# Large neighbour aggregation: ScalarE's Abs in two halves, with the second copy of a tile between them

## The reference, cut to what matters

```
thr = mean - std                       # of the distances to the half-rolled image
xj = 0
for axis in (rows, columns):
    for s in range(0, size, K):        # K = 4 at level 0, 2 at the others
        xr = roll(x, s, axis)
        dist = sum over channels |x - xr|
        m = dist < thr
        xj = maximum(xj, (xr - x) * m)
```

## Time and profile before

| | us |
|---|---|
| median of 3 timed runs | 8505.98 |
| the profiled execution | 8487.06 |
| its span, first to last instruction | 8485.2 |
| PE busy | 5984.2 |
| DVE busy | 5096.2 |
| ACT busy | 4346.2 |
| POOL busy | 3214.9 |

### The profile page before, as it was taken

The page is one execution under the profiler, slowest core; times in us unless marked ns, Lnnn a source line. Parts: engine busy times, 40 slices in busy tenths (PEclk is TensorE's granted clock), DMA queues, the critical chain, the costliest instruction groups (busy, mean ns, idle before and its releaser), DMA issues. The chain is left out here.

```text
span 8485.2 us, 82873 instructions
## 1 busy us (share of the span) xinstructions
PE 5984.2 (71%) x26092; PEld 2959.6 (35%) x26286; DVE 5096.2 (60%) x5868; ACT 4346.2 (51%) x4790; POOL 3214.9 (38%) x1140
## 2 busy tenths in 40 slices
PE   7896577667776676985676432363998849889798
PEld 5673111111111111334111111252886627666263
DVE  2111799899999898650799654224222223459596
ACT  1123699899999898750899311101001121125657
POOL 0161799899999897000898031000000000000000
PEclk9998899999999999998999766586999979999898
DMA  6567330111211101667000322255547879984545
GB/s 124 131 199 238 59 40 20 40 60 21 40 20 25 65 30 35 192 160 145 24 11 1 105 45 50 42 90 157 103 85 126 149 188 170 188 171 126 181 124 186
DMA packets 1476784, 841.70 MB, mean 99 GB/s; under 512 B 638754, under 2 KB 1406264, under 8 KB 1462664
## 3 DMA queue, kind: packets, MB, share of 16 engines
q1 hardware_dynamic: 1261032, 717.18, 36.9%
q10 hardware_dynamic: 215456, 120.95, 6.0%
HBM read 533.33 MB, written 304.65 MB: 99 GB/s over the span
## 5 line engine op out<-in xcount | busy, mean ns | idle before, releaser
L1025 POOL TENSOR_TENSOR ag_D<-ag_X 128x2048 f32<-128x2048 f32 (+15 forms) x940 | 2907.7, 3127 | 1060.9 <-DMA ag_X<-h 941.8
L1089 PE MATMUL ag_slot<-ag_S,ag_w 128*128 128x512 bf16 x4768 | 1470.7, 389 | 838.7 <-DVE ag_J L1131 720.9
L1131 DVE TENSOR_TENSOR ag_J<-ag_J,ag_slot 128x1024 f32<-128x1024 f32 x1240 | 1454.7, 1214 | 153.4 <-PE ag_slot L1089 72.9
L1138 DVE SCALAR_TENSOR_TENSOR ag_J<-ag_slot,ag_J 128x1024 f32<-128x1024 f32 (+14 forms) x1640 | 1436.4, 928 | 0.0
L1056 ACT ACTIVATE ag_slot<-ag_D 128x1024 f32<-128x1024 f32 x1280 | 1308.5, 1025 | 173.8 <-DVE ag_J L1138 58.9
L1040 ACT ACTIVATE ag_A<-ag_D 128x2048 f32<-128x2048 f32 x640 | 1212.1, 1894 | 0.0
L1089 PEld LDWEIGHTS ag_slot<-ag_S,ag_w 128*128 128x128 bf16 x4960 | 286.5, 98 | 2256.7 <-DVE ag_J L1131 1299.8
L1082 PE MATMUL ag_dist<-ag_A,ag_given 128*32 128x512 f32 x5120 | 698.5, 618 | 101.6 <-ACT ag_A L1040 77.6
L255 PE MATMUL dc_ps<-dc_high,dc_w_high 128*128 128x512 f32 (+1 forms) x1056 | 425.2, 403 | 281.2 <-DVE dc_low L68 281.2
L1048 ACT ACTIVATE ag_S<-ag_dist,ag_limit 128x512 bf16<-128x512 f32 x640 | 486.7, 761 | 2.3 <-PE ag_dist L1082 2.3
L269 ACT ACTIVATE dc_out<-dc_ps,shift,scale 128x512 f32<-128x512 f32 (+1 forms) x88 | 67.4, 766 | 818.2 <-PE dc_ps L255 818.2
(11 more groups left out here) (208 smaller groups left out, 9521.9 us busy)
## 6 DMA issues: line engine op xcount, KB each, us to landing
ag_X<-h SPq DMA_DIRECT2D x18, 2048.0 KB, 13.3
xj<-ag_J SPq DMA_DIRECT2D x18, 2048.0 KB, 7.2
c_mul<-gated SPq DMA_DIRECT2D x64, 512.0 KB, 11.5
wa_x<-r SPq DMA_DIRECT2D x128, 256.0 KB, 2.9
u<-wa_x SPq DMA_DIRECT2D x128, 256.0 KB, 2.4
mn_x<-u SPq DMA_DIRECT2D x64, 512.0 KB, 5.7
cpe_band<-in_band SPq DMA_DIRECT2D x16, 1792.0 KB, 8.0
gr_hj<-h SPq DMA_DIRECT2D x168, 128.0 KB, 2.8
```

The source lines that it names most:

```text
L1025: pool.tensor_tensor(self.tile_part(self.d[u % self.DEPTH][:], u, piece), self.span(g, axis, there, there + hi - lo), self.span(g, axis, l ...
L1089: mm = self.nc.tensor.matmul(self.slot[v % self.SLOTS][:, b, :], self.w[:, weights + 2 * h + b, :], self.s[u % 3][:], start=False, stop=Tr ...
L1131: dve.tensor_tensor(best, best, new, ALU.max).then_inc(self.dve_steps, 1)
L1138: dve.scalar_tensor_tensor(out=best, in0=self.slot_part(v, lo, hi), scalar=-1.0, in1=best, op0=ALU.mult, op1=ALU.max)\
```

## The change

ScalarE's Abs becomes two ACTIVATEs of 1024 elements. In `act_unit` the first goes ahead of the second copy, the second behind it. Each half keeps the waits of the whole and counts up the semaphore `absed` by one, and TensorE's distance waits for both.

```diff
-            self.act_abs(act, u)
+            self.act_abs(act, u, 0)
+            self.act_abs(act, u, 1)
...
-    def act_abs(self, act, u):
+    def act_abs(self, act, u, h):
         act.wait_ge(self.diffed, self.diffs_to[u])
         reach(act, self.summed, u - 2)
-        act.activation(self.a[u % 3][:], self.d[u % self.DEPTH][:], ACT.Abs).then_inc(self.absed, 1)
+        part = slice(h * self.SUB, (h + 1) * self.SUB)
+        act.activation(self.a[u % 3][:, part], self.d[u % self.DEPTH][:, part], ACT.Abs).then_inc(self.absed, 1)
...
         self.act_copy(act, 2 * u + 1)
+        if u + self.LEAD < len(self.units):
+            self.act_abs(act, u + self.LEAD, 0)
         if u + 1 < len(self.units):
             self.act_copy(act, 2 * u + 2)
         if u + self.LEAD < len(self.units):
-            self.act_abs(act, u + self.LEAD)
+            self.act_abs(act, u + self.LEAD, 1)
         if u + 1 < len(self.units):
             self.act_sign(act, u + 1)
...
     def pe_dist(self, pe, u):
-        pe.wait_ge(self.absed, u + 1)
+        pe.wait_ge(self.absed, 2 * u + 2)
```

## The result

The median after the change is 8463.8 us (5 runs, 8454.7 to 8470.61); the kernel before, in five runs beside it, has 8507.99 (8499.84 to 8519.72). The ratio is 0.9946, 95% interval 0.9931 to 0.996: 44 us less, 8461 was predicted.

What follows compares the result with a forecast made beforehand. DVE was taken to wait 0.21 us a pair behind a loop through ScalarE's second copy and Abs. 150 row pairs x 0.14 plus 150 column pairs x 0.16 save 45 us: 8506 to 8461, range 8449 to 8500.

Steps and rivals of the forecast that it cites:

- DVE's hidden wait of 0.21 us: DVE's two plain rolls take 2.47 us a pair of units instead of 2.26; without waiting, 9.11 in rows, 9.18 in columns.
- The loop: Roll end, second copy, Abs, distance, pad, Max: 4.64 us, then 4.68 to the roll's end, setting the measured pair of 9.32.
- The price of a half: On ScalarE, half an Abs takes 1.04 us, holding a 0.945 us slot; a unit grows 0.09 to 4.44 us.
- The new loop: After the change, from the first copy's slot: 5.66 us to Max, then 3.48 or 3.55: 9.14 or 9.21 a pair.
- TensorE's order: Distance matmuls stand behind the two swaps, which wait for the second Max: 9.16 us a pair in rows, 9.23 in columns.
- POOL's floor: POOL's own pace in the large aggregations: 9.16 us a pair in rows, 9.22 in columns.
- The sum: 150 row pairs at 0.14 us and 150 column pairs at 0.16 us saved: 45 us.
- The borders: At chunk borders nothing changes: the second copy's vanished wait of about 0.1 us pays the halves' added 0.09.
- The signs of being wrong: Wrong if: half over 1.06 us or gaps; two rolls still 2.47; POOL's 2048-element difference slower; a border over 0.5 us longer.
- Partial saving: Rival: POOL slows under pressure or PE's order costs more; 0.08 us a pair, 24 us saved, 8482; chance 0.18.
- halves that eat the gain: Rival: second copy's wait goes but halves at 1.056 us without overlap eat it; 10 us saved, 8496; chance 0.15.
- ScalarE as the pace: Rival: ScalarE becomes the pace once both halves exceed 2.11 us; at a 1.26 slot 234 us slower, 8740; chance 0.12.

Runs made afterwards that it cites:

- e10: e2 with Abs first on ScalarE, ahead of both copies, and the distance first on TensorE, ahead of pad and swaps: 8428.01 us, ratio 0.9921.
- e1: The changed kernel with both halves of Abs behind the second copy: 8521.14 us, ratio 1.003 to the kernel before.
- e5: The changed kernel with each half of Abs cut again in place, the distance waiting for four: 8518.07 us, ratio 1.0021 to the kernel before.
- e9: The same kernel as e2, run on another chip: 8452.73 us, ratio 0.9939 to the kernel before.
- e7: e2 with POOL's one-piece differences computed over their first half only, from a stage's sixth unit on: 8446.72 us, ratio 0.9934.
- e11: e10 with the edit of e7, POOL's one-piece differences over their first half only: 8420.56 us, ratio 0.9915.
- e2: The kernel before with Abs in one piece moved ahead of the second copy: 8450.96 us, ratio 0.9943.

## Why the prediction was right

- **What bounds the kernel.** DVE's hidden wait of 0.21 us in every pair, read from starts alone, was right: e10, in which the wait is gone, has the 9.11 and 9.18 that were worked out for DVE.
- **The loop.** Roll end, second copy, Abs, distance, pad, Max is shown: its Abs made 0.09 longer made the pair 0.10 longer (e1), and the halves cut again cost 0.18 to 0.19 (e5). The new loop was put at 5.66 + 3.48 = 9.14 and, with the split roll, 9.21. The trace has slots of 0.96, 0.95 and 0.95 where 0.945 was taken, and 1108.02 - 1106.33 = 1.69 where 1.70 was: 0.02 more in all, 9.16 and 9.23.
- **The price of a half.** 1041 ns against 1.04 us. A further cut cost 0.09 us in e1 and in e5. The Trainium skill, page "ScalarE: Activation LUTs", section "What ACT_TABLE_LOAD costs", states 186 ns + 0.833 ns per element and an overlap of some 93 ns; estimated by it, a half takes 1039 ns and a further cut costs 186 - 93 = 93 ns. The traces agree with both.
- **What is late next.** Of the three floors, TensorE's order (9.16 and 9.23) was right: 9.17 and 9.24, with Abs out of the loop (e9) and with POOL relieved (e7); with the distance ahead of the swaps it goes (e10). POOL's floor was right in rows (9.18 in three chunks of e10, against 9.11 in e11) and too high in columns: 9.22 was read from a stretch where POOL waited for ScalarE's copies, and e10 runs columns at 9.18.
- **The sum.** 45 us was predicted, and the aggregations gave 39.8. I split that: the first 14 pairs with rolls of each pass, added up over the ten row passes, went from 1306.7 to 1294.6 us, so 12.1, where 140 x 0.14 = 19.6 was meant; over the column passes from 1314.7 to 1295.9, 18.8 for 140 x 0.16 = 22.4. In rows 7.5 us are missing: 3.2 in the second half of a pass, 9.24 where the sum had 9.18, and 3.4 in first pairs, three of which take 10.9 us where one did before (last section). The 3.6 missing in columns are for the most part one such first pair and five pairs of 9.51. The lone units, the last pairs and the borders gave the other 8.9, where I had counted 3.0 for the last pairs. The medians differ by 44 us, so the total came closer than its terms.
- **The borders.** They were called unchanged. Of the 8.9 us, 6.9 are lone units (188.1 to 181.2 over all passes): a stretch of lower clock that fell into them before falls into the first pair now in some passes, and is shorter or gone in others. Lone units and first pairs together went from 376.9 to 372.1 us, 4.8 less, of which the pairs' saving was to give 3.0. So the starts of passes are about even, but not one by one: some grew by up to 1.8 us, and others shrank by up to 1.4.
- **The signs of being wrong.** Two of those listed showed and yet decided nothing: POOL's difference of 2048 elements is 17 ns slower, but in e7 a POOL with idle time leaves the pair at 9.17; and some borders grew by more than 0.5 us, but the sum of all didn't grow.
- **The rivals.** Partial saving (8482) and halves that eat the gain (8496) lie outside the five runs. ScalarE as the pace was refuted by e5 more than by the time: with four Abs instructions a unit it still wasn't the pace.
- **What I hadn't asked.** The prediction took the split for the means of the gain. It is the order: e1, the split without the move, costs 0.3%, and e2, the move without the split, has the whole gain. So the prediction was right in the loop and in the time, and had too narrow a view of what takes Abs out of the loop.

## What to carry to other kernels

When three engines look full and the views of waits show nothing, add up the steps from start to start on the last engine, find the two equal instructions that take longer than their peers, and follow the start times back from there to a loop that closes. On an engine that works in order, first try another order: an instruction that can wait goes behind those that are ready and feed a longer chain, and a split, which costs 0.09 us a cut here, is for where no whole instruction can be moved. After each step compute what is late next, and check it by relieving that resource alone: e7 cleared POOL, and e10 then gained by reordering TensorE, and ScalarE with it.

## What the runs showed of the hardware

TensorE's granted clock falls to 0.50 at the start of most passes (18 of the changed kernel's 20, 19 of the 20 before), and the work beside it can take longer. Where it stays there over some 6 us of the first pair with rolls, that pair takes 10.9 us instead of 9.17 or 9.24: in 4 passes of the changed kernel and in 5 of e9 (10.9 to 11.0). The kernel before has one, but its clock falls earlier, in the lone units (a distance of 1.94 us at 2607.40, at a granted clock of 0.50), eight of which take 10.1 to 10.4 us where the others take 8.3 to 9.7. I can't tie it to the order of the work. TensorE alone, at the border of a column chunk of the changed kernel, and then the windows of the same stretch (the column before DMA share and GB/s is the granted clock, as a share of 2.4 GHz):

```profile
1840.62 1.07 PE L1086 MATMUL ag_dist<-ag_A,ag_given 128*32 128x512 f32 x8
...
1845.21 1.07 PE L1086 MATMUL ag_dist<-ag_A,ag_given 128*32 128x512 f32 x8 [2.26 <-ACT ag_A L1042]
...
1849.66 1.06 PE L1086 MATMUL ag_dist<-ag_A,ag_given 128*32 128x512 f32 x8 [2.26 <-ACT ag_A L1042]
...
1854.71 1.94 PE L1086 MATMUL ag_dist<-ag_A,ag_given 128*32 128x512 f32 x8
...
1858.93 0.60 PE L1093 MATMUL ag_slot<-ag_S,ag_w 128*128 128x512 bf16 x2 [0.67 <-DVE ag_J L1135]
```

```profile
1842.00:1848.00 6.00, 3.02 (x16) 0.50 (x14) 3.79 (x5) 6.00 (x8) 6.00 (x3) 1.00 0.95 350
1848.00:1853.00 5.00, 2.83 (x12) 0.53 (x14) 2.86 (x4) 5.00 (x6) 5.00 (x3) 0.81 0.88 367
1853.00:1856.00 3.00, 2.91 (x12) 0.33 (x10) 3.00 (x5) 2.65 (x4) 3.00 (x1) 0.50 1.02 437
```

TensorE waited twice for 2.26 us for ScalarE's Abs; then the granted clock fell from 1.00 to 0.50 (1.2 GHz), the distance took 1.94 us instead of 1.07, and by 1858.93 the swaps were back at 0.60. In the same stretch the DMA engines were nearly full (0.88 to 1.02); whether that has a part in it isn't shown.
